# Low-part rotary scores as pairs of 64-row matmuls in a macaron attention kernel

## The chip, the core and the metric

The kernel runs on one core of one Trainium2 chip. The metric is the device time of one execution in microseconds, lower is better. Three runs of the kernel before gave 2384.84, 2382.19 and 2379.25 us, median 2382.19 us.

## What is computed

Four sequences of 512 tokens (width 1024) go through half a feed-forward block (a router over 8 experts with rank 16), an attention block, and half a feed-forward block again. The attention is of the latent kind: 32 heads, each query of 128 unrotated and 64 rotated dimensions, keys and values made from a latent of 128, one rotated key of 64 dimensions for all heads.

```python
q_pe = _apply_rope(q_pe, cos[None, :, None, :], sin[None, :, None, :])
k_pe = _apply_rope(k_pe, cos[None, :, :], sin[None, :, :])
scores = (jnp.einsum('bshd,bthd->bhst', q_nope, k_nope) + jnp.einsum('bshd,btd->bhst', q_pe, k_pe)) * scale
scores = jnp.where(causal[None, None], scores, jnp.finfo(scores.dtype).min)
probs = jax.nn.softmax(scores, axis=-1)
out = jnp.einsum('bhst,bthd->bshd', probs, v).reshape(b, s, NH * V_DIM)
```

## The kernel before

Every product is made from numbers split in a high and a low part (both fp32r), as high by high, high by low and low by high. The order of all work is written out by hand, for each engine in its own block, with counting semaphores between them.

The sequences are treated in two pairs (`p` = 0 and 1). For each pair, attention runs over 16 groups `g` of two heads. A group has four slots `k` = 0 to 3: `h = k % 2` is the head, `b = k // 2` the sequence of the pair. So there are 2 x 16 x 4 = 128 slots. Group 0 is written out in `first_body`, groups 1 to 14 are a loop over `body`, group 15 is `body` with `last`.

A slot computes scores for four query tiles `i` = 0 to 3 of 128 queries. Tile `i` is causal: it meets `(i + 1) * 128` keys, so its matmuls have 128, 256, 384 and 512 columns. It goes to PSUM bank `i % 2` (`bank_s`). Five matmuls make a tile: three for the unrotated part (`keyT`), and two for the rotated part (`ropeT`). For the rotated part, `qst` stacks the high part of the rotated query (64 rows) over its low part (64 rows), and `ropeT` holds the 64 rows of the key twice, so one matmul over 128 rows does high and low of the query against one part of the key. The first takes the key's high part, the second its low part. They are the fourth and fifth matmul of the tile, and both use the same weights.

Between the score tiles of slot `k`, TensorE does other work of the slot before it, in the order of `slot`: scores 0 and 1; the transposes of probabilities 0 and 1; output matmuls (six of 512 columns); scores 2; transposes 2; outputs; scores 3; transposes 3; projections ("fills"); outputs; values; outputs.

When a tile's scores are there, VectorE adds the mask on the diagonal (L1771) and takes the row maximum (L1773), and ScalarE takes the exponential out of the bank, with the row sum read by an accumulator instruction of its own that carries the semaphore `exp_done` (L1369). A score tile may start when its bank is free: tile `i` waits until the exponential of tile `i - 2` is done (L937). DVE's L1794 adds an output tile to the residual.

The stacked queries are made by DMA. After the rotation on GpSimd (`rope_r`), SyncE issues in `stack_halves` four DMAs, one per head and part, each 64 partitions by 512 numbers, into `qst[b]`. TensorE waits for them before scores 0 of slots 0 and 2 (`qst_in`).

In the profile the line of nearly all matmuls is that of a helper (L646, `products`); they are told apart by their tiles: `ps<-keyT,arena` and `ps<-ropeT,arena` are score matmuls.

Of the kernel before, what the change touches and what calls it, by code (L numbers as in the profile page):

```python
# [7 lines left out]
F32 = mybir.dt.float32  # L8
# [3 lines left out]
P = 128  # L12
# [5 lines left out]
def build_macaron(nc, x, wzkv, qnorm, kvnorm, wqn, wpe, wk, wv, wo, ra, rb, bm,  # L18
# [9 lines left out]
    SEQ = c_pos.shape[2]  # L28
    NPAIR = TOK // SEQ // 2
    NT = 2 * SEQ // P  # L30
# [8 lines left out]
    NG = NH // 2  # L39
# [19 lines left out]
    NF = [NT, 2 * NT, NT]  # L59
    U0 = [0, 2 * NT, 5 * NT]  # L60
# [22 lines left out]
    with ExitStack() as ctx:  # L83
        def sb(name, shape, dt=F32):
            return ctx.enter_context(nc.sbuf_tensor(name, shape, dt))

        def sem(name):
            return ctx.enter_context(nc.semaphore(name))
# [4 lines left out]
        ropeT = sb("ropeT", [P, 2, PAIR], F32R)  # L93
# [43 lines left out]
        rope_r = arena(W0 + 2 * QL, 2, SEQ)  # L137
# [4 lines left out]
        qst = [arena(X0, 2, SEQ), arena(8 * D, 2, SEQ)]  # L142
# [70 lines left out]
        def bank_s(i):  # L213
            return ps[:, i % 2, :]
# [32 lines left out]
        xt_hi = sem("xt_hi")  # L247
        xt_lo = sem("xt_lo")
# [30 lines left out]
        scores_done = sem("scores_done")  # L279
        masked = sem("masked")  # L280
        max_ready = sem("max_ready")
        exp_done = sem("exp_done")
# [11 lines left out]
        qst_in = sem("qst_in")  # L294
# [4 lines left out]
        y_added = sem("y_added")  # L299

        block = ctx.enter_context(nc.Block())
        GATE_STEPS = 13

        def lat_at(s, i):
# [16 lines left out]
        def slot_n(p, g, k):  # L321
            return (p * NG + g) * 4 + k

        def settle(eng):

            eng.sem_inc(settled, 1)
# [50 lines left out]
        def q_slot(p, g, k, first, last):  # L377

            if first and k < 2:
                a, d = PRO[p][f"q{k}"]  # L380
            elif k:
                a, d = q_events(p, last, first)[f"q{k}"]
            else:
                a, d = q_events(p, False)["q0"]
                a, d = a - EV[p], d - EVD[p]
            return qbase(p, g) + a + 1, qbase_d(p, g) + d + 1
# [23 lines left out]
        def _(sp):  # L410
# [124 lines left out]
            def swap_halves():  # L535
                for q in range(4):
                    o = q ^ 1
                    sp.dma_start(rope_f[32 * q:32 * q + 32, 1, :], rope_f[32 * o:32 * o + 32, 0, :])\
                      .then_inc(swap_in, 16)

            def stack_halves(n, b, used):
                sp.wait_ge(rope_ready, n + 1)
                settle(sp)
                if used is not None:
                    sp.wait_ge(scores_done, used)
                    settle(sp)
                for h in range(2):
                    for part in range(2):
                        dst = 64 * (part ^ h)
                        sp.dma_start(qst[b][dst:dst + 64, h, :].bitcast(F32),  # L550
                                     rope_r[64 * h:64 * h + 64, part, :].bitcast(F32)).then_inc(qst_in, 16)
                sp.wait_ge(qst_in, 64 * (n + 1))
                settle(sp)

            def attention(p):
# [86 lines left out]
        def _(pe):  # L642
# [7 lines left out]
            def three(w_hi, w_lo, m_hi_, m_lo_):  # L650
                return [(w_hi, m_hi_), (w_hi, m_lo_), (w_lo, m_hi_)]
# [273 lines left out]
            def scores(p, g, k, i, first, last):  # L925

                h, b = k % 2, k // 2
                n = slot_n(p, g, k)
                if i == 0:

                    a, d = q_slot(p, g, k, first, last)
                    pe.wait_ge(q_act, a)
                    pe.wait_ge(q_dve, d)
                    if h == 0:
                        pe.wait_ge(qst_in, 64 * (p * 2 * NG + 2 * g + b + 1))
                if not (first and k == 0 and i < 2):
                    pe.wait_ge(exp_done, 4 * n + i - 1)  # L937
                elif i == 0:

                    pe.wait_ge(xt_hi, U0[p] + NF[p] + NT)  # L940
                    pe.wait_ge(xt_lo, U0[p] + NF[p] + NT)
                qs = slice(i * P, (i + 1) * P)
                ks = slice(b * SEQ, b * SEQ + (i + 1) * P)
                dst = bank_s(i)[:, 0:(i + 1) * P]
                products(dst, three(qT[h][:, 0, qs], qT[h][:, 1, qs], keyT[:, 0, ks], keyT[:, 1, ks])
                         + [(qst[b][:, h, qs], ropeT[:, 0, ks]), (qst[b][:, h, qs], ropeT[:, 1, ks])])\
                    .then_inc(scores_done, 1)

            def turn_probs(n, k, i, first):

# [165 lines left out]
        def _(act):  # L1116
# [53 lines left out]
            def gates(c):  # L1170
                act.wait_ge(gate_chain, c * GATE_STEPS + 3)
                ts = slice((c % 2) * HT, (c % 2 + 1) * HT)
                nc.scalar.activation(lgt[:, 1, ts], lgt[:, 0, ts], ACT.Exp).then_inc(gate_exp, 1)
# [247 lines left out]
            def drained(p, s):  # L1421
                n = all_slots(p) - 1
                for i in range(NS):
                    turned(n, i)
                norm_ffn(s, 0)

                act.wait_ge(qst_in, 64 * (p + 1) * 2 * NG)
                split_ra(s)
                valued(n, 3)
                norm_ffn(s, 1)  # L1430
                turned_ffn(s, 0)

                act.wait_ge(y_done, y_n(p, NG, 1))
                turned_ffn(s, 1)
                norm_ffn(s, 2)
                for i in range(5):
                    keep_h(F0[s] + i)
                    turned_ffn(s, i + 2)
                    if i == 3:
                        gates((F0[s] + i) // HT)  # L1440
                    norm_ffn(s, i + 3)
                    if i == 0:
                        split_bm(s)
# [31 lines left out]
        def _(dve):  # L1475
# [31 lines left out]
            def gates(c, stage_):  # L1507

                first = (0, 3, 8, GATE_STEPS)
                step = [first[stage_]]  # L1510
                base = c * GATE_STEPS

# [406 lines left out]
        def _(pool):  # L1919
# [58 lines left out]
            def rotate(n, a_wait, first=False, between=None):  # L1978

                step = [4 * n]  # L1980

                def link(ins):
                    step[0] = step[0] + 1
                    ins.then_inc(rope_chain, 1)
                    pool.wait_ge(rope_chain, step[0])
                    settle(pool)
                pool.wait_ge(q_act, a_wait)
                settle(pool)
                if not first:

                    pool.wait_ge(qst_in, 64 * n)
                    settle(pool)
                link(G.tensor_tensor(rope_f[:, 2, :], rope_f[:, 0, :], pos_tab[:, 0, :], ALU.mult))  # L1993
                if between is not None:
                    between()
                pool.wait_ge(swap_in, 64 * (n + 1))
                settle(pool)
                link(G.tensor_tensor(rope_f[:, 1, :], rope_f[:, 1, :], pos_tab[:, 1, :], ALU.mult))  # L1998
                link(G.tensor_tensor(rope_r[:, 0, :], rope_f[:, 2, :], rope_f[:, 1, :], ALU.add))
                link(G.tensor_tensor(rope_f[:, 2, :], rope_f[:, 2, :], rope_f[:, 1, :], ALU.add))  # L2000
                G.tensor_tensor(rope_r[:, 1, :], rope_f[:, 2, :], rope_r[:, 0, :].bitcast(F32),
                                ALU.subtract).then_inc(rope_ready, 1)
# [111 lines left out]
```

## Time and profile before

| | |
|---|---|
| median of three runs | 2382.19 us |
| the profiled execution | 2382.79 us |
| its span, first to last instruction | 2380.7 us |
| mean granted TensorE clock | 0.989 |
| TensorE matmul busy | 2318.6 us (97%), 12832 matmuls |
| VectorE busy | 1627.7 us (68%) |
| ScalarE busy | 950.4 us (40%) |
| GpSimd busy | 521.3 us (22%) |
| score matmuls on `ropeT` | 1024 |
| DMAs that stack queries | 256, of 128 KB |

Matmul records overlap one another since matmuls are pipelined: how fast TensorE goes is read from the distance of starts, not from durations. PEld rows are the weight loads that belong to the matmuls, one each. A row of the timeline merges neighbours of one kind: its start is that of the first, its duration runs to the end of the last.

### The profile page before, as it was taken

Reading aid. Unit: us, or ns where it says so; the run is one execution under the profiler, and the core shown is the slowest. Engines: PE = TensorE matmul, PEld = TensorE weight load, DVE = VectorE, ACT = ScalarE, POOL = GpSimd, SP = SyncE. Lnnn points to the kernel's source line nnn. Section 1 sums busy time; section 2 is a strip of 40 time slices with the busy share of each in tenths; the row PEclk is TensorE's granted clock in tenths of the full one; section 3 lists DMA queues with packets and bytes.
Section 4 is the critical chain, followed back from the end, with each engine's and each line's share of the span. In section 5 each row is a group of like instructions: output and inputs, shape, how many; then the busy total and the mean of one; then the engine's idle time right before and its main releaser. Section 6 shows DMA issues by size and latency. Waiting matters only on the chain.

```text
span 2380.7 us, 40789 instructions
## 1 busy us (share of the span) xinstructions
PE 2318.6 (97%) x12832; PEld 1992.7 (84%) x12832; DVE 1627.7 (68%) x3581; ACT 950.4 (40%) x2311; POOL 521.3 (22%) x568
## 2 busy tenths in 40 slices
PE   8989999999999999999998989999999999999999
PEld 7977888888888888888888868888888888888888
DVE  6656666676666676666776556666666666666676
ACT  5533334443343344433444433333333333333343
POOL 4222221112222111222132222222222222222211
PEclk9999999999999999999999989999999999999999
DMA  4023333332223333333221212222222222222221
GB/s 150 17 68 108 107 103 102 106 97 80 95 74 97 105 104 106 107 107 95 96 90 64 66 44 79 78 78 78 78 78 78 78 78 78 78 78 78 75 67 72
DMA packets 101050, 203.45 MB, mean 85 GB/s; under 512 B 12544, under 2 KB 40704, under 8 KB 98944
## 3 DMA queue, kind: packets, MB, share of 16 engines
q1 hardware_dynamic: 79488, 156.55, 21.9%
q10 hardware_dynamic: 21504, 46.14, 5.9%
q8 instruction: 35, 0.57, 0.1%
q14 instruction: 23, 0.19, 0.0%
HBM read 97.78 MB, written 54.53 MB: 64 GB/s over the span
## 4 chain that ended last, share of the span: by engine, by line
PE 89%; DVE 3%; DMA 3%; ACT 2%; POOL 1%; issue 1%; SPq 1%; ACTq 0%; DVEq 0%; POOLq 0%
PE ps L646 74%; PE ps L956 6%; PE ps L714 4%; PE ps L915 2%; PE ps L660 1%; DVE arena L1477 1%; PE ps L921 1%; DMA kept_out<-arena 1%; ACT arena L1118 1%; PE ps L1086 1%; DVE stats L1486 1%; DMA out<-xacc 1%; DMA xacc<-in_x 0%; DMA arena<-arena 0%; DMA stage<-stage 0%
## 5 line engine op out<-in xcount | busy, mean ns | idle before, releaser
L646 PE MATMUL ps<-arena 128*128 128x512 f32 (+1 forms) x4032 | 966.7, 380 | 3.4 <-DVE arena L1477 1.5
L1477 DVE TENSOR_TENSOR arena<-ps,arena 128x384 fp32r<-128x384 f32 (+4 forms) x920 | 549.2, 601 | 508.8 <-ACT arena L1118 502.8
L1118 ACT ACTIVATE arena<-ps 128x384 fp32r<-128x384 f32 (+4 forms) x920 | 470.1, 527 | 868.6 <-PE ps L646 459.5
L646 PEld LDWEIGHTS ps<-arena 128*128 128x128 f32 x4032 | 677.1, 190 | 122.5 <-issue 9.4
L646 PE MATMUL ps<-zT,arena 128*128 128x512 f32 x1728 | 450.5, 405 | 2.8 <-issue 1.4
L1369 ACT ACTIVATE stage<-ps,negmax 128x128 f32<-128x128 f32 (+3 forms) x512 | 270.7, 529 | 366.4 <-DVE negmax L1773 362.5
L1794 DVE TENSOR_TENSOR xacc<-ps,xacc 128x512 f32<-128x512 f32 x512 | 351.7, 687 | 82.3 <-PE ps L646 73.8
L646 PEld LDWEIGHTS ps<-zT,arena 128*128 128x128 f32 x1728 | 318.5, 190 | 73.5 <-issue 3.8
L1993 POOL TENSOR_TENSOR stage<-stage,pos_tab 128x512 f32<-128x512 f32 x64 | 82.7, 1292 | 1294.7 <-ACT stage L1118 1287.7
L646 PE MATMUL ps<-keyT,arena 128*128 128x128 f32 (+3 forms) x1536 | 351.2, 337 | 9.0 <-ACT stage L1369 5.5
L646 PEld LDWEIGHTS ps<-keyT,arena 128*128 128x128 f32 x1536 | 260.7, 191 | 66.6 <-issue 22.4
L646 PEld LDWEIGHTS ps<-arena,lat 128*128 128x128 f32 x1536 | 247.5, 190 | 36.1 <-ACT arena L1118 5.9
L646 PE MATMUL ps<-arena,lat 128*128 128x512 f32 (+3 forms) x1536 | 260.6, 319 | 5.8 <-ACT arena L1118 5.1
L1773 DVE TENSOR_REDUCE negmax<-ps 128x1 f32<-128x128 f32 (+3 forms) x512 | 251.5, 491 | 17.5
L646 PE MATMUL ps<-ropeT,arena 128*128 128x128 f32 (+3 forms) x1024 | 247.5, 323 | 0.0
L956 PE MATMUL ps<-ident,stage 128*128 128x128 f32 x1280 | 203.6, 273 | 4.6 <-DVE arena L1477 3.7
L1771 DVE TENSOR_TENSOR ps<-ps,mask 128x128 f32<-128x128 f32 x512 | 150.7, 294 | 59.1 <-PE ps L646 59.1
L646 PEld LDWEIGHTS ps<-ropeT,arena 128*128 128x128 f32 x1024 | 174.0, 191 | 11.5
L956 PEld LDWEIGHTS ps<-ident,stage 128*128 128x128 f32 x1280 | 158.2, 141 | 28.5 <-DVE stage L1783 4.9
L1783 DVE TENSOR_SCALAR stage<-stage,rrec 128x128 f32<-128x128 f32 (+3 forms) x512 | 165.7, 388 | 4.5
L1998 POOL TENSOR_TENSOR stage<-stage,pos_tab 128x512 f32<-128x512 f32 x64 | 82.5, 1288 | 177.3 <-DMA stage<-stage 177.3
L714 PE MATMUL ps<-arena 128*128 128x288 f32 x768 | 110.7, 299 | 5.1 <-ACT stage L1118 2.7
(86 smaller groups left out, 1311.3 us busy)
## 6 DMA issues: line engine op xcount, KB each, us to landing
arena<-arena SPq DMA_DIRECT2D x256, 128.0 KB, 2.3
kept_out<-arena SPq DMA_DIRECT2D x16, 2048.0 KB, 6.3
arena<-kept_out ACTq DMA_DIRECT2D x32, 1024.0 KB, 5.6
stage<-stage SPq DMA_DIRECT2D x256, 64.0 KB, 2.0
stage<-in_wo SPq DMA_DIRECT2D x16, 1024.0 KB, 6.1
kept_q<-arena SPq DMA_DIRECT2D x16, 768.0 KB, 7.4
arena<-kept_q ACTq DMA_DIRECT2D x32, 384.0 KB, 3.1
out<-xacc SPq DMA_DIRECT2D x15, 512.0 KB, 2.7
```

The costliest lines, as they stand in the source:

```text
L646: last = nc.tensor.matmul(dst, w, m, start=start and n == 0, stop=stop and n == len(passes) - 1, skip_group_check=skip)
L714: last = nc.tensor.matmul(bzs[half], xnT[:, b, xp, k * P:(k + 1) * P], w_lat[:, wp, k, half * ZH:(half + 1) * ZH], start=(k == 0 and c == ...
L956: last = nc.tensor.transpose(bank_t(i)[:, j * P:(j + 1) * P], prob[:, k % 2, poff(i) + j * P:poff(i) + (j + 1) * P], ident[:, :])
L1118: return nc.scalar.activation(dst, src, ACT.Copy)
L1369: nc.scalar.activation(prob[:, k % 2, poff(i):poff(i + 1)], bank_s(i)[:, 0:(i + 1) * P], ACT.Exp, bias=negmax[:, k % 2, i:i + 1], accum_ou ...
L1477: return nc.vector.tensor_tensor(dst, src, part.bitcast(F32), ALU.subtract)
L1771: nc.vector.tensor_tensor(diagonal, diagonal, mask[:, :], ALU.add).then_inc(masked, 1)
L1773: nc.vector.tensor_reduce(negmax[:, k % 2, i:i + 1], bank_s(i)[:, 0:(i + 1) * P], AX_X, ALU.max, negate=True).then_inc(max_ready, 1)
L1783: nc.vector.tensor_scalar(pr, pr, rrec[:, k % 2, i:i + 1], None, ALU.mult).then_inc(prob_ready, 1)
L1794: nc.vector.tensor_tensor(xs, bank_y(j), xs, ALU.add).then_inc(y_added, 1)
L1993: link(G.tensor_tensor(rope_f[:, 2, :], rope_f[:, 0, :], pos_tab[:, 0, :], ALU.mult))
L1998: link(G.tensor_tensor(rope_f[:, 1, :], rope_f[:, 1, :], pos_tab[:, 1, :], ALU.mult))
```

## The change

The matmul with the key's low part is cut from 128 rows to 64: it takes only the high part of the query (low by low is no longer computed). For two neighbouring tiles `i` and `i + 1` the two 64-row matmuls are issued one behind the other, ahead of all else of the pair. One uses rows 0 to 63 of the array, the other rows 64 to 127. So that both find the query's high part in their rows, the DMAs that stack the queries swap the halves for odd query tiles; there are now eight DMAs, each of 64 partitions by two runs of 128 numbers, and `qst_in` counts to 128 for each stack. As both tiles of a pair are started at once, the even tile waits until both banks are free, that is for the exponential of tile `i - 1`, and the odd tile has no wait of its own.

```diff
+            def every_other(ap, odd):
+                return ap.bitcast(F32).rearrange("p (t o s) -> p t o s", o=2, s=P)[:, :, odd, :]
...
                 for h in range(2):
                     for part in range(2):
-                        dst = 64 * (part ^ h)
-                        sp.dma_start(qst[b][dst:dst + 64, h, :].bitcast(F32),
-                                     rope_r[64 * h:64 * h + 64, part, :].bitcast(F32)).then_inc(qst_in, 16)
-                sp.wait_ge(qst_in, 64 * (n + 1))
+                        for odd in range(2):
+                            dst = 64 * (part ^ h ^ odd)
+                            sp.dma_start(every_other(qst[b][dst:dst + 64, h, :], odd),
+                                         every_other(rope_r[64 * h:64 * h + 64, part, :], odd)).then_inc(qst_in, 16)
+                sp.wait_ge(qst_in, QST * (n + 1))
...
-                if not (first and k == 0 and i < 2):
-                    pe.wait_ge(exp_done, 4 * n + i - 1)
-                elif i == 0:
-                    pe.wait_ge(xt_hi, U0[p] + NF[p] + NT)
-                    pe.wait_ge(xt_lo, U0[p] + NF[p] + NT)
+                if i % 2 == 0:
+                    if not (first and k == 0 and i == 0):
+                        pe.wait_ge(exp_done, 4 * n + i)
+                    else:
+                        pe.wait_ge(xt_hi, U0[p] + NF[p] + NT)
+                        pe.wait_ge(xt_lo, U0[p] + NF[p] + NT)
+                    for o in range(2):
+                        rows = slice(64 * (h ^ o), 64 * (h ^ o) + 64)
+                        t = i + o
+                        nc.tensor.matmul(bank_s(t)[:, 0:(t + 1) * P], qst[b][rows, h, t * P:(t + 1) * P],
+                                         ropeT[rows, 1, b * SEQ:b * SEQ + (t + 1) * P], start=True, stop=False)
...
                 products(dst, three(qT[h][:, 0, qs], qT[h][:, 1, qs], keyT[:, 0, ks], keyT[:, 1, ks])
-                         + [(qst[b][:, h, qs], ropeT[:, 0, ks]), (qst[b][:, h, qs], ropeT[:, 1, ks])])\
-                    .then_inc(scores_done, 1)
+                         + [(qst[b][:, h, qs], ropeT[:, 0, ks])], start=False).then_inc(scores_done, 1)
```

On TensorE, in the loop body of pair 0, the stretch from scores 1 of a slot to scores 3 stands as follows before (L646 is a matmul of `products`, L956 a transpose, L937 the register of the wait for the bank):

```order
L646 MATMUL ps<-keyT,arena 128x256 x3
L646 MATMUL ps<-ropeT,arena 128x256 x2
L951 ISA
L953 REGISTER_ALU
L956 MATMUL ps<-ident,stage 128x128
L951 REGISTER_ALU
L956 MATMUL ps<-ident,stage 128x128 x2
L991 ISA
L646 MATMUL ps<-arena 128x512 x6
L937 REGISTER_ALU
L646 MATMUL ps<-keyT,arena 128x384 x3
L646 MATMUL ps<-ropeT,arena 128x384 x2
```

And the same stretch with the change (lines have moved: L957 is the new 64-row matmul, L654 `products`, L972 the transpose, L947 the register of the wait):

```order
L654 MATMUL ps<-keyT,arena 128x256 x3
L654 MATMUL ps<-ropeT,arena 128x256
L967 ISA
L969 REGISTER_ALU
L972 MATMUL ps<-ident,stage 128x128
L967 REGISTER_ALU
L972 MATMUL ps<-ident,stage 128x128 x2
L1007 ISA
L654 MATMUL ps<-arena 128x512 x6
L947 REGISTER_ALU
L957 MATMUL ps<-ropeT,arena 128x384
L957 MATMUL ps<-ropeT,arena 128x512
```

The fifth matmul of each tile has gone, and those of tiles 2 and 3 stand in front of tile 2's others, behind the wait.

On SyncE, in `first_body` of pair 0, the swaps of halves (`stage<-stage`), the loads of output weights and the two stacks (`arena<-arena`) stand before as:

```order
L538 DMA stage<-stage 32x512 x4
L445 DMA stage<-in_wv 128x2x128
L446 DMA stage<-in_wo 128x2x1024
L550 DMA arena<-arena 64x512 x4
L538 DMA stage<-stage 32x512 x4
L550 DMA arena<-arena 64x512 x4
L459 DMA kept_out<-arena 128x4096
```

and with the change as:

```order
L539 DMA stage<-stage 32x512 x4
L446 DMA stage<-in_wv 128x2x128
L447 DMA stage<-in_wo 128x2x1024
L558 DMA arena<-arena 64x2x128 x8
L539 DMA stage<-stage 32x512 x4
L558 DMA arena<-arena 64x2x128 x8
L460 DMA kept_out<-arena 128x4096
```

Eight issues stand for each stack where there were four, with half the bytes each.

## Rows read from the trace of the kernel before

**Rows 1.** The page, part 1: busy time, share, instructions.
```profile
PE 2318.6 (97%) x12832; PEld 1992.7 (84%) x12832; DVE 1627.7 (68%) x3581; ACT 950.4 (40%) x2311; POOL 521.3 (22%) x568
```

**Rows 2.** Groups by line and shape: busy us, mean ns; idle before.
```profile
L646 PE MATMUL ps<-ropeT,arena 128*128 128x512 f32 x256 | 80.9, 397 | 0.0
```

**Rows 3.** Timeline, one slot's score tiles: start us, us, what.
```profile
1569.10 0.39 PE L646 MATMUL ps<-ropeT,arena 128*128 128x128 f32 x2
1569.32 0.57 PE L646 MATMUL ps<-keyT,arena 128*128 128x256 f32 x3
...
1569.73 0.39 PE L646 MATMUL ps<-ropeT,arena 128*128 128x256 f32 x2
...
1569.96 0.49 PE L956 MATMUL ps<-ident,stage 128*128 128x128 f32 x3
...
1570.20 1.64 PE L646 MATMUL ps<-arena 128*128 128x512 f32 x6
...
1571.68 0.68 PE L646 MATMUL ps<-keyT,arena 128*128 128x384 f32 x3
...
1572.20 0.51 PE L646 MATMUL ps<-ropeT,arena 128*128 128x384 f32 x2
...
1572.55 0.49 PE L956 MATMUL ps<-ident,stage 128*128 128x128 f32 x3
...
1574.96 0.63 PE L646 MATMUL ps<-ropeT,arena 128*128 128x512 f32 x2
...
1575.44 0.60 PE L956 MATMUL ps<-ident,stage 128*128 128x128 f32 x4
```

**Rows 4.** Timeline of the same slot: VectorE, ScalarE, and tile 2's first load.
```profile
1569.02 0.69 DVE L1794 TENSOR_TENSOR xacc<-ps,xacc 128x512 f32<-128x512 f32 x1
...
1569.63 0.29 DVE L1771 TENSOR_TENSOR ps<-ps,mask 128x128 f32<-128x128 f32 x1
...
1569.95 0.29 DVE L1773 TENSOR_REDUCE negmax<-ps 128x1 f32<-128x128 f32 x1
...
1570.16 0.30 DVE L1771 TENSOR_TENSOR ps<-ps,mask 128x128 f32<-128x128 f32 x1
...
1570.49 0.42 DVE L1773 TENSOR_REDUCE negmax<-ps 128x1 f32<-128x256 f32 x1
...
1570.95 0.48 ACT L1369 ACTIVATE stage<-ps,negmax 128x256 f32<-128x256 f32 x1 [0.22 <-DVE negmax L1773]
1571.32 0.19 ACT L1369 ACTIVATION_READ_ACCUMULATOR stage<-ps,negmax 128x1 f32 x1
...
1571.45 0.59 PEld L646 LDWEIGHTS ps<-keyT,arena 128*128 128x128 f32 x3
```

**Rows 5.** Timeline, the same place in slot 3 of pair 0.
```profile
320.05 0.19 ACT L1369 ACTIVATION_READ_ACCUMULATOR stage<-ps,negmax 128x1 f32 x1
...
320.84 0.19 PEld L646 LDWEIGHTS ps<-keyT,arena 128*128 128x128 f32 x1 [0.24 <-issue]
```

**Rows 6.** Timeline near the end: six matmuls, a load among them held up.
```profile
2373.93 1.56 PE L646 MATMUL ps<-arena 128*128 128x512 f32 x6
...
2374.74 0.53 PEld L646 LDWEIGHTS ps<-arena 128*128 128x128 f32 x3 [0.16 <-DVE xacc L1578]
```

**Rows 7.** Part 6 of the page: DMA issues, count, KB, us to landing.
```profile
arena<-arena SPq DMA_DIRECT2D x256, 128.0 KB, 2.3
```

**Rows 8.** Timeline of the stack DMAs, steady state.
```profile
1559.24 2.43 SPq L550 DMA_DIRECT2D arena<-arena  x4
```

**Rows 9.** Timeline of a stack in the first group of pair 0, and the load that needs it.
```profile
165.37 2.42 SPq L550 DMA_DIRECT2D arena<-arena  x4
170.41 0.19 PEld L646 LDWEIGHTS ps<-keyT,arena 128*128 128x128 f32 x1 [0.24 <-issue]
```

**Rows 10.** Timeline of a stack in the second group, and the matmul that needs it.
```profile
229.82 2.41 SPq L550 DMA_DIRECT2D arena<-arena  x4
```

**Rows 11.** Timeline of TensorE behind it.
```profile
235.18 0.55 PE L646 MATMUL ps<-keyT,arena 128*128 128x128 f32 x3 [1.64 <-DMA arena<-arena]
```

More of the change, by code:

```diff
@@ L301, in build_macaron @@
         block = ctx.enter_context(nc.Block())
+        QST = 128
         GATE_STEPS = 13
@@ L934, in scores @@
                     if h == 0:
-                        pe.wait_ge(qst_in, 64 * (p * 2 * NG + 2 * g + b + 1))
-                if not (first and k == 0 and i < 2):
-                    pe.wait_ge(exp_done, 4 * n + i - 1)
-                elif i == 0:
-                    pe.wait_ge(xt_hi, U0[p] + NF[p] + NT)
-                    pe.wait_ge(xt_lo, U0[p] + NF[p] + NT)
+                        pe.wait_ge(qst_in, QST * (p * 2 * NG + 2 * g + b + 1))
+                if i % 2 == 0:
[9 more added lines that the diff above has]
+                                         ropeT[rows, 1, b * SEQ:b * SEQ + (t + 1) * P], start=True, stop=False)
                 qs = slice(i * P, (i + 1) * P)
@@ L1425, in drained @@
                 norm_ffn(s, 0)
-                act.wait_ge(qst_in, 64 * (p + 1) * 2 * NG)
+                act.wait_ge(qst_in, QST * (p + 1) * 2 * NG)
                 split_ra(s)
@@ L1989, in rotate @@
                 if not first:
-                    pool.wait_ge(qst_in, 64 * n)
+                    pool.wait_ge(qst_in, QST * n)
                     settle(pool)
```

## The prediction

> **What bounds the kernel now.** I read part 1 of the page first. TensorE's matmuls are busy for 97% of the span, VectorE comes next with 68% [rows 1]. So a matmul that is taken out counts, and a stall of TensorE counts in full. The groups by line and shape come next: there are four groups of score matmuls on the rotated key, for 128, 256, 384 and 512 columns, with 256 instances each, and the last stands in [rows 2]. Two for each tile in 128 slots make 256. The half with the key's low part, 128 of each size, is what the change works on. Durations in that view overlap (397 ns for 512 columns), so what a matmul costs I take from distances of starts in the timeline of one slot. Two of 128 columns: 1569.10 to 1569.32, 0.11 us each. Two of 256: 1569.73 to 1569.96, 0.115 each. Two of 384: 1572.20 to 1572.55, 0.175 each. Two of 512: 1574.96 to 1575.44, 0.24 each [rows 3]. Note that 128 and 256 columns cost the same: there the weight load is the pace, 0.11 us for each. Last I read what VectorE and ScalarE do between the second and third score tile [rows 4], since the change makes the third wait for them, and the DMAs that stack the queries [rows 7 to 11].
>
> **The pairs themselves.** No matmul goes away: five loads and five matmuls for a tile stay. The gain can only come from two 64-row matmuls running side by side.
>
> Tiles 2 and 3: before, 0.175 + 0.24 = 0.415 us for the two low parts. The trace of before holds no 64-row matmul, so I bound. Fully side by side, the pair costs its longer one, 0.24, and 0.175 is saved. If the second starts one load pace (0.11) behind the first, it costs 0.35, and 0.065 is saved. If they run one behind the other nothing is saved; that is a rival below. Between the first two I have no nearer row for either, and take the middle, 0.12. Times 128 slots: 15.4 us, from 8.3 to 22.4.
>
> The Trainium skill, "TensorE: Matmul & The Clock Gate", section "Measured speedup vs the span model", gives a pack of row tiles the duration of one matmul plus some 4 ns for each further tile. By it the pair would cost 0.244 us and the gain would be 0.171 x 128 = 21.9 us, near my upper end. No row of before can show it.
>
> Tiles 0 and 1: both are paced by loads, and both loads remain. 0 to 0.11 us for a slot, but only where it can be kept: it brings tile 2 forward by as much, and tile 2 now has to wait (next part). So it counts only in slot 3 of pair 0, 16 slots, where a fill stands in between: 16 x 0.055 = 0.9 us, from 0 to 1.8.
>
> **The new wait.** Tile 2 used to need the exponential of tile 0; now it needs that of tile 1. Queued behind the waiting load is all of TensorE. In the timeline the chain to that exponential is tight: an addition of the output before (L1794) starts at 1569.02 when its matmuls are done, and from there VectorE goes without a gap: mask 1569.63, maximum 1569.95, mask 1570.16, maximum 1570.49; then the exponential 1570.95, and its accumulator read 1571.32 to 1571.51, which carries the semaphore. Tile 2's first load starts at 1571.45 and its matmul at 1571.68 [rows 3, 4]. So the load comes 0.06 us before what it will have to wait for. A handover costs about 0.04 (maximum over at 1570.91, exponential at 1570.95), so the load moves to about 1571.55, 0.10 late. Does that move the matmul? The six output matmuls before it started at 1570.20 and are streaming until then. Near the end of the kernel a load among six such matmuls was held up so that its engine idled 0.16 us, and the six still took 1.56 us, which is five paces of 0.234 and one duration of 0.39 [rows 6]: it was hidden. So I take nearly nothing, 0.025 us. The other bound: after the wait the load's full lead of 0.23 (1571.45 to 1571.68) is needed again, the matmul starts at 1571.78, 0.10 late. In slot 3 of pair 0 the read ends at 320.24 and the load starts at 320.84 [rows 5], a margin of 0.6. That leaves 112 slots: 2.8 us, from 0 to 11. And what tiles 0 and 1 gain there is waited away, since VectorE's chain starts from the output before and does not move.
>
> Tile 0 now waits for tile 3 of the slot before, whose scores start at about 1575 in a slot that begins at 1569, some 7 us ahead of the next slot: no cost. VectorE, ScalarE and GpSimd do the same work as before.
>
> **The stacks.** Each stack has eight issues for four. Four take 2.43 us, so eight take 4.9, and the last starts some 2.5 us later. Bytes are the same. In steady state the last issue starts about 1.8 us after 1559.24, lands 2.3 us later at about 1563.4, and is needed just before 1569.1: margin over 5 us, nothing lost [rows 3, 7, 8]. In the first groups it is not so. Issued from 165.37, a stack lands at about 169.5 and is needed at 170.41, a margin of 0.9 [rows 7, 9]; the next stack has the same. Each then comes 1.6 us late. The one after, issued at 229.82, already holds TensorE for 1.64 us until 235.18 [rows 10, 11], and one at the start of pair 1 does so too: 2.5 us late each. TensorE has nothing to put there, since its order is fixed. 2 x 1.6 + 2 x 2.5 = 8.2 us, lost. I keep 6 to 12 as bounds, since shorter runs of 512 bytes may land later.
>
> **Changing between 128 and 64 rows.** There are four changes in a slot (into the pair and out of it, twice), 512 in all. The nearest row for none is the change from matmul to transpose at 1569.96, at the common pace of 0.11 [rows 3]: price 0. The nearest row for a dear one is the load in [rows 5], before which the load engine idled 0.24 us for nothing the profile shows, behind a matmul of another kind: 0.24 less the pace of 0.11 is 0.13 for each, 66 us in all. I take 0 in the sum, because most neighbours of different kinds in the timeline follow at pace, and keep the rest as a rival.
>
> **The sum.** -15.4 - 0.9 + 2.8 + 8.2 = -5.3 us, against the profiled execution's 2382.79, which lies 0.6 above the median of the runs: 2377.5, or 2377 against the median. Its own range, with all bounds to one side: 2382.8 - 22.4 - 1.8 + 6 = 2365, and 2382.8 - 8.3 + 11 + 12 = 2397.
>
> **The rivals.**
>
> A toll at each change of rows, which makes it slower. The engine must empty before matmuls of another row count go in, or the load can't be fetched ahead of it. For it speaks only [rows 5]; against it, that changes of weights, tile and kind cost nothing elsewhere. At 0.08 us, two thirds of the bound, 512 x 0.08 = 41 us on top of the sum: 2418, from 2395 to 2443. From 0.01 us for each change it eats the gain, and from 0.02 the kernel is slower. The Trainium skill, "TensorEngine Tiling (Array Packing)", section "Key Properties", says that changing the tiling mode, unlike changing the tile, drains the engine; it gives no price, and the trace of before, with one mode throughout, cannot show it. That is the page that speaks against this change.
>
> The pair does not overlap, so the change doesn't do what it says: the sum without 15.4 and 0.9, that is 2382.8 + 11.0 = 2394.
>
> The wait is dearer. The scores of tile 0 now end as the sixth matmul of the slot and not the fifth, one pace of 0.11 later; if VectorE's chain starts from them rather than from the addition, the load is 0.21 late. Beyond about 0.12 a late load is no longer hidden, so it decides from there: 0.1 x 112 = 11 us more, 2389.
>
> **Chances.** A measurement of this kernel can tell 0.2%, or 4.8 us, from no change: faster is below 2377.4, slower above 2387.0.
> - The sum as worked out, 0.50: it lies on the border, so 0.29 faster, 0.17 same, 0.04 slower.
> - The toll, 0.31: 0.30 slower, 0.01 same.
> - No overlap, 0.08: all but 0.01 slower.
> - The dearer wait, 0.11: 0.02 faster, 0.03 same, 0.06 slower.
>
> Together 0.31 faster, 0.22 same, 0.47 slower. The likeliest single case is the first, so the time is 2377. For 8 in 10 the range must reach into the toll: 2364 to 2438.
>
> **What the new profile would show.** Right: the starts of the two 64-row matmuls of tiles 2 and 3 lie 0 to 0.11 us apart, and the next one on `keyT` comes 0.24 to 0.35 after the first; PEld shows idle time before the pair of tiles 2 and 3 in 112 slots, released by ScalarE's L1369, below 0.15 us each, but the matmul's start does not move; the waits for the stack DMAs grow from two to four or more, together by about 8 us; nothing idles at the first `keyT` load behind a pair. Wrong: a gap of some 0.1 us at each entry into and exit from a pair (toll), 0.4 us from the first to the end of the pair (no overlap), or TensorE idle before tile 2 by 0.1 us or more in most slots (dearer wait). The forecast fails if any of these three is there, or if the stacks in the first groups are late by much more than 2.5 us.

## The result: 3.4% slower, and the profile after

The changed kernel takes 2462.55 us (median of four runs, 2461.22 to 2465.67). The kernel before took 2383.15 beside it. The ratio is 1.0339, with a 95% interval of 1.0325 to 1.0354: 79 us slower. The forecast was 2377, its range ended at 2438, and the time lies outside it. Of the four cases the one called "a toll at each change of rows" came true, and it is dearer than I had let it be.

Part 1 and two lines of part 5 of the page after (L957 is the new 64-row matmul; the column behind the bar is busy us, mean ns, then idle time before it):

```profile
PE 2385.2 (97%) x12832; PEld 1945.0 (79%) x12832; DVE 1653.9 (67%) x3581; ACT 949.6 (39%) x2311; POOL 520.8 (21%) x568
...
L957 PEld LDWEIGHTS ps<-ropeT,arena 64*128 64x128 f32 x512 | 48.0, 184 | 118.9 <-issue 71.1
L957 PE MATMUL ps<-ropeT,arena 64*128 64x128 f32 (+3 forms) x512 | 114.0, 413 | 21.7 <-ACT stage L1385 11.0
```

The number of matmuls is that of [rows 1], and TensorE is again busy for 97% of a longer span. Busy shares do not show the loss, since the records of matmuls last longer than their distances: the last output matmul below has a record of 0.40 us, and the next matmul starts 0.32 us after it, so the record covers the gap. What shows the loss is 118.9 us of idle time of the load engine before just 512 loads. Before 226 of the 256 pairs it is one stretch of 0.36 us, 81 us in all. Before 16 more it is 0.76 us, 12 us in all: these are tiles 2 and 3 of slot 3 in pair 0, which stand behind a fill. The last 26 us are 12 stretches of 0.65 to 4.5 us in the first groups of both pairs, the waits for stacks among them.

The timeline of TensorE at tiles 0 and 1 of a steady slot of pair 1, which answers to [rows 3]:

```profile
1591.05 0.39 PE L654 MATMUL ps<-arena 128*128 128x512 f32 x1
1591.37 0.39 PE L957 MATMUL ps<-ropeT,arena 64*128 64x128 f32 x2
1591.69 0.55 PE L654 MATMUL ps<-keyT,arena 128*128 128x128 f32 x3
1592.08 0.27 PE L654 MATMUL ps<-ropeT,arena 128*128 128x128 f32 x1
1592.19 0.57 PE L654 MATMUL ps<-keyT,arena 128*128 128x256 f32 x3
1592.60 0.28 PE L654 MATMUL ps<-ropeT,arena 128*128 128x256 f32 x1
1592.72 0.49 PE L972 MATMUL ps<-ident,stage 128*128 128x128 f32 x3
```

and of tiles 2 and 3, with the last output matmul ahead:

```profile
1594.20 0.40 PE L654 MATMUL ps<-arena 128*128 128x512 f32 x1
1594.53 0.49 PE L957 MATMUL ps<-ropeT,arena 64*128 64x384 f32 x2
1594.95 0.78 PE L654 MATMUL ps<-keyT,arena 128*128 128x384 f32 x3
1595.58 0.34 PE L654 MATMUL ps<-ropeT,arena 128*128 128x384 f32 x1
1595.75 0.49 PE L972 MATMUL ps<-ident,stage 128*128 128x128 f32 x3
```

The rows of the pairs hold two matmuls in 0.39 and 0.49 us. In the groups by shape a single 64-row matmul of 256 columns has a mean of 386 ns and one of 512 columns 498 ns, so both of a pair start together. The side-by-side run works. But from the last output matmul to the pair pass 0.32 us where 0.234 is usual, and from the pair to the next matmul 0.32 and 0.42 us, where a single matmul of the longer size would take 0.11 and 0.24.

The loads of the same place:

```profile
1591.37 0.19 PEld L957 LDWEIGHTS ps<-ropeT,arena 64*128 64x128 f32 x2 [0.35 <-issue]
1591.69 0.41 PEld L654 LDWEIGHTS ps<-keyT,arena 128*128 128x128 f32 x3
```

Before, tile 2's first load starts at 1571.45, together with the last output matmul and 0.23 ahead of its own [rows 4]. Now each first load behind a change starts together with its own matmul. It is not fetched ahead, in either direction. So a change costs twice: the load comes later behind the matmul before it than the next matmul usually would, and then it stands uncovered. That it waits until the array is empty is how I read the first part; the experiment with one 64-row matmul in each tile bears on it. From the starts of single matmuls in the two traces, from the last output matmul to the first transpose: tiles 0 and 1 took 1.37 us together and take 1.67; tile 2 took 1.10 and takes 1.55; tile 3, which has lost a matmul, took 1.40 and takes 1.17. Together 0.5 us more for a slot.

Waits of the load engine, and TensorE's waits for the stacks (us in total, times, longest):

```profile
PEld ps L957 <- issue: 71.1, 147, 4.5
PEld ps L654 <- issue: 64.0, 237, 1.6
PEld ps L957 <- ACT stage L1385: 45.8, 108, 2.4
...
PEld ps L654 <- DVE arena L1493: 9.2, 28, 0.4
```

```profile
PE ps L957 <- DMA arena<-arena: 10.8, 4, 4.3
```

The third line needs care. The profile puts 45.8 us to the exponential that a pair waits for. Here is that read, and the pair's load:

```profile
1594.09 0.19 ACT L1385 ACTIVATION_READ_ACCUMULATOR stage<-ps,negmax 128x1 f32 x1
...
1594.53 0.19 PEld L957 LDWEIGHTS ps<-ropeT,arena 64*128 64x128 f32 x2 [0.36 <-ACT stage L1385]
```

The read is over at 1594.28 and the load starts only at 1594.53, 0.25 us later, whereas a handover costs 0.04. The load at tiles 0 and 1, whose semaphore was there long before (`[0.35 <-issue]`), comes just as long after the output matmul: 0.32 against 0.33. So the idle time is named after the last semaphore, and would be there without it.

### The profile page after: what moved, and what is told of

Same layout as the page of the kernel before. It is cut to its first block, busy times and chain, and to the rows that moved or that the text cites. A ratio compares the mean times of both kernels' runs of the same rounds, so it can differ in the third digit from the quotient of the medians.

```text
span 2459.4 us, 41129 instructions
## 1 busy us (share of the span) xinstructions
PE 2385.2 (97%) x12832; PEld 1945.0 (79%) x12832; DVE 1653.9 (67%) x3581; ACT 949.6 (39%) x2311; POOL 520.8 (21%) x568
## 4 chain that ended last, share of the span: by engine, by line
PE 87%; DVE 4%; DMA 2%; ACT 2%; POOL 1%; SPq 1%; issue 1%; ACTq 0%; DVEq 0%; POOLq 0%
PE ps L654 70%; PE ps L972 5%; PE ps L722 4%; PE ps L957 4%; PE ps L923 2%; DVE arena L1493 2%; PE ps L668 1%; ACT arena L1134 1%; PE ps L929 1%; SPq L558 1%; DVE stats L1502 1%; DMA xacc<-in_x 1%; DMA stage<-stage 0%; ACT stage L1148 0%; DMA out<-xacc 0%
## 5 line engine op out<-in xcount | busy, mean ns | idle before, releaser
L654 PE MATMUL ps<-arena 128*128 128x512 f32 (+1 forms) x4032 | 967.1, 381 | 3.9 <-DVE arena L1493 1.5
L654 PEld LDWEIGHTS ps<-arena 128*128 128x128 f32 x4032 | 677.6, 190 | 123.0 <-issue 9.7
L654 PE MATMUL ps<-zT,arena 128*128 128x512 f32 x1728 | 449.2, 404 | 5.3 <-issue 2.8
L654 PEld LDWEIGHTS ps<-zT,arena 128*128 128x128 f32 x1728 | 317.7, 190 | 80.2 <-DVE arena L1493 9.2
L654 PE MATMUL ps<-keyT,arena 128*128 128x128 f32 (+3 forms) x1536 | 365.4, 351 | 0.0
L654 PEld LDWEIGHTS ps<-keyT,arena 128*128 128x128 f32 x1536 | 241.9, 191 | 76.4 <-issue 47.1
L654 PEld LDWEIGHTS ps<-arena,lat 128*128 128x128 f32 x1536 | 246.5, 189 | 33.5 <-issue 4.2
L654 PE MATMUL ps<-arena,lat 128*128 128x512 f32 (+3 forms) x1536 | 259.3, 318 | 3.3 <-ACT arena L1134 1.9
L972 PE MATMUL ps<-ident,stage 128*128 128x128 f32 x1280 | 204.6, 274 | 4.5 <-DVE arena L1493 3.7
L972 PEld LDWEIGHTS ps<-ident,stage 128*128 128x128 f32 x1280 | 159.8, 141 | 28.3 <-DVE stage L1799 4.7
L654 PE MATMUL ps<-ropeT,arena 128*128 128x128 f32 (+3 forms) x512 | 167.0, 326 | 0.0
L957 PEld LDWEIGHTS ps<-ropeT,arena 64*128 64x128 f32 x512 | 48.0, 184 | 118.9 <-issue 71.1
L957 PE MATMUL ps<-ropeT,arena 64*128 64x128 f32 (+3 forms) x512 | 114.0, 413 | 21.7 <-ACT stage L1385 11.0
```

Of the source, the lines that this page charges most:

```text
L654: last = nc.tensor.matmul(dst, w, m, start=start and n == 0, stop=stop and n == len(passes) - 1, skip_group_check=skip)
L957: nc.tensor.matmul(bank_s(t)[:, 0:(t + 1) * P], qst[b][rows, h, t * P:(t + 1) * P], ropeT[rows, 1, b * SEQ:b * SEQ + (t + 1) * P], start=T ...
L972: last = nc.tensor.transpose(bank_t(i)[:, j * P:(j + 1) * P], prob[:, k % 2, poff(i) + j * P:poff(i) + (j + 1) * P], ident[:, :])
```

## The experiments

All ratios are against the kernel before on the same chip, with 95% intervals; its median beside the first four experiments was 2381.48 us, beside the next three 2381.53, and beside the last two 2382.26 and 2382.16. "Loop of pair 0" is the time for a group of four slots, worked out from the starts of the first `keyT` matmul of group 3 and group 15, divided by 12: 64.47 before, 66.97 with the change. The same in pair 1: 59.43 and 61.47.

**Full rows.** The changed kernel with 128-row matmuls in the place of the 64-row ones.

```diff
-                        rows = slice(64 * (h ^ o), 64 * (h ^ o) + 64)
+                        rows = slice(0, P)
```

> The changed kernel, with its order, waits and eight stack DMAs, but the moved low-part matmuls use all 128 rows again, so no matmul has another row count than its neighbours. My theory (each change of row count empties the engine and leaves the next weight load uncovered, some 0.2 us for each of 512 changes): the toll goes with the 64 rows; what is left over the kernel before are the stacks, about 8 us, and a wait that a late load hides: 2390 to 2397 us, and the load engine idles less than 0.15 us before tile 2. Rival A (the order and the new wait for the exponential, to which the profile puts 45.8 us of idle time of the load engine, are the cost): it stays above 2430. Rival B (the 64-row matmuls do not run together): it would lose nothing by this edit against the changed kernel, 2450 to 2470, since tile 3 has a matmul less anyway.

Measured: 2404.24 us, ratio 1.0093 (1.0078 to 1.0109). The 64 rows carry 58 of the 79 us, and rival A falls. But 22.8 us are left, not 8 to 15, so the forecast for this run was missed by 7 us. The place of the wait, in the timeline of this kernel:

```profile
1593.62 1.64 PE L654 MATMUL ps<-arena 128*128 128x512 f32 x6
1595.00 0.30 PEld L957 LDWEIGHTS ps<-ropeT,arena 128*128 128x128 f32 x2 [0.17 <-ACT stage L1385]
1595.10 0.58 PE L957 MATMUL ps<-ropeT,arena 128*128 128x384 f32 x2
```

From the six output matmuls to the next pass 1.48 us, as before (1570.20 to 1571.68 [rows 3]). The load engine has idled 0.17 us before it, a little more than the 0.15 of the forecast, and the matmul is not late. Rival B falls too.

**The DMAs alone.** The kernel before with the eight stack DMAs.

```diff
-                        dst = 64 * (part ^ h)
-                        sp.dma_start(qst[b][dst:dst + 64, h, :].bitcast(F32),
-                                     rope_r[64 * h:64 * h + 64, part, :].bitcast(F32)).then_inc(qst_in, 16)
...
+                        for odd in range(2):
+                            dst = 64 * (part ^ h ^ odd)
+                            sp.dma_start(every_other(qst[b][dst:dst + 64, h, :], odd),
+                                         every_other(rope_r[64 * h:64 * h + 64, part, :], odd)).then_inc(qst_in, 16)
...
```

> The kernel before, with only the stack DMAs of the change: eight of 64 KB for four of 128 KB, halves swapped for odd tiles, which 128-row matmuls do not mind. My theory: 2.5 us later for each stack, which costs only in the first groups, 7 to 9 us in all: 2390 to 2392. Rival (runs of 512 bytes disturb or delay more than that in the steady state): above 2397. Rival (a loss in the first groups is made up later): 2383 to 2385.

Measured: 2391.87 us, ratio 1.0046 (1.0032 to 1.0060), 10.4 us. TensorE's waits for stacks in it:

```profile
PE ps L652 <- DMA arena<-arena: 10.1, 4, 4.1
```

These are four waits of 10.1 us in all, where there were two of 3.4 us, one of them that of [rows 11]: 6.7 us more. Both loops run at their old 64.47 and 59.43 us. From the first score to the start of the fourth group this trace takes 3.5 us more in pair 0 and 2.9 us more in pair 1. So what the trace shows of the loss, 6.4 us, is in the first groups. The profiled execution (2388.14 us) is the fastest of five, and the median lies 3.7 us above it; the two slowest have a granted clock of 0.986 against its 0.989. Where the rest of the 10.4 us arises, no trace shows.

**Both of a pair in the same half.**

```diff
-                        rows = slice(64 * (h ^ o), 64 * (h ^ o) + 64)
+                        rows = slice(64 * h, 64 * h + 64)
```

> The changed kernel, but both matmuls of a pair use the same 64 rows, so they cannot run side by side (for the odd tile these rows hold the low part of the query, so another part of the sum is computed). As many changes of row count as in the changed kernel. My theory: inside one row count the second load is covered and matmuls follow at the usual pace, so the pair gets longer by one load pace 0.11 us (tiles 0 and 1) and by one matmul of 384 columns, 0.17 us (tiles 2 and 3): 0.28 x 128 = 36 us more, 2490 to 2505 us; starts inside the pair 0.11 and 0.17 us apart instead of 3 ns. Rival (the pair does not really overlap in the changed kernel, starts are only stamped together): 2460 to 2466, no difference. Rival (a second tile in use costs too): below 2480.

Measured: 2497.84 us, ratio 1.0490 (1.0474 to 1.0506), 35.3 us above the changed kernel; the forecast was 36. The two pairs in its timeline:

```profile
1595.97 0.49 PE L957 MATMUL ps<-ropeT,arena 64*128 64x128 f32 x2
...
1596.39 0.55 PE L654 MATMUL ps<-keyT,arena 128*128 128x128 f32 x3
...
1599.24 0.67 PE L957 MATMUL ps<-ropeT,arena 64*128 64x384 f32 x2
...
1599.83 0.79 PE L654 MATMUL ps<-keyT,arena 128*128 128x384 f32 x3
```

0.42 and 0.59 us from pair to next, against 0.32 and 0.42: side by side saves 0.10 and 0.17 us. One detail of the forecast was off: the starts inside the pairs are 0.17 and 0.28 us apart and not 0.11 and 0.17, since the record of the first matmul begins with its uncovered load. And since this kernel has full rows' order and waits and nothing side by side, its distance to full rows is the toll by itself: 2497.84 - 2404.24 = 93.6 us, 0.183 us for each of 512 changes. In the loops, where nothing else waits, it is 0.194: (68.07 - 64.96) / 16 in pair 0 and (62.60 - 59.49) / 16 in pair 1. The first three groups of pair 0 take only 3.4 us more than with full rows in the traces, and not 3 x 3.1; there TensorE waits for stacks as well.

**96 rows.** The pair's matmuls on rows 0 to 95, not split in halves.

```diff
-                        rows = slice(64 * (h ^ o), 64 * (h ^ o) + 64)
+                        rows = slice(0, 96)
```

> The changed kernel, but the moved matmuls use 96 rows of the array, 0 to 95, for both tiles, so they do not use all rows but are issued as matmuls of the full array (for the odd tile other terms are summed). My theory, the toll is for leaving the full-array form and not for idle rows: as with all 128 rows, 2390 to 2397 us. Rival (any matmul with fewer active rows than its neighbour pays): 2455 or more, with two full matmuls one behind the other even 2490.

Measured: 2404.27 us, ratio 1.0095 (1.0080 to 1.0110), the time of full rows (2404.24) well within the noise; the loops agree too, 64.97 and 59.49 us against 64.96 and 59.49. So 32 idle rows cost nothing, and going to 64 rows does. The range I gave was missed by the same 7 us as in full rows.

**One 64-row matmul in each tile.** The kernel before, in its order.

```diff
-                         + [(qst[b][:, h, qs], ropeT[:, 0, ks]), (qst[b][:, h, qs], ropeT[:, 1, ks])])\
+                         + [(qst[b][:, h, qs], ropeT[:, 0, ks]),
+                            (qst[b][64 * h:64 * h + 64, h, qs], ropeT[64 * h:64 * h + 64, 1, ks])])\
```

> The kernel before in order, waits and stack DMAs, but the fifth matmul of each score tile uses only the 64 rows that hold the high part of the query. Nothing runs side by side, and each of the 512 tiles goes to 64 rows and back: 1024 changes of row count, twice those of the changed kernel. My theory: each change costs what the first runs gave, (2497.8 - 2404.2) / 512 = 0.18 us, so 2382 + 187 = 2569 us, 2555 to 2590. Rival (the toll hangs on a matmul that starts in another half of the rows or on a pair, not on the change of row count): below 2480. Rival (the toll is for time waited before a pair, since a pair starts behind a wait): below 2420.

Measured: 2534.42 us, ratio 1.0646 (1.0626 to 1.0667). 153 us for 1024 changes, 0.149 each. Both rivals fall, but the time is 21 us below the theory's range: the price of a change is not the same everywhere. The timeline at tiles 0 and 1:

```profile
1591.56 0.53 PE L646 MATMUL ps<-ropeT,arena 128*128 128x128 f32 x2
1592.02 0.61 PE L646 MATMUL ps<-keyT,arena 128*128 128x256 f32 x3
1592.47 0.59 PE L646 MATMUL ps<-ropeT,arena 128*128 128x256 f32 x2
1592.99 0.55 PE L957 MATMUL ps<-ident,stage 128*128 128x128 f32 x3
```

and at tile 3:

```profile
1598.40 0.82 PE L646 MATMUL ps<-ropeT,arena 128*128 128x512 f32 x2
...
1598.72 0.18 PEld L646 LDWEIGHTS ps<-ropeT,arena 64*128 64x128 f32 x1 [0.36 <-issue]
1599.14 0.42 PEld L957 LDWEIGHTS ps<-ident,stage 128*128 128x128 f32 x4 [0.24 <-issue]
1599.15 0.66 PE L957 MATMUL ps<-ident,stage 128*128 128x128 f32 x4
```

The entry is 0.32 again, 0.09 above the usual 0.234. Behind matmuls of 128, 256 and 384 columns it is 0.21, 0.21 and 0.26 us, where 0.11, 0.11 and 0.17 are usual: again 0.09 more. So this part of the price does not depend on how long the matmul before is, which fits a load that waits until the array is empty.

I compare starts with those of the kernel before, tile by tile, as medians of 28 slots in the loop of pair 1. Tile 0, the one whose exit leads to products, takes 0.29 us more; tiles 1, 2 and 3, whose exits lead to transposes, take 0.34 us more each. Together this is 1.31 us for a slot, and the loop shows the same, (64.68 - 59.43) / 4 = 1.31. Two changes of the pairs above cost 2 x 0.194 = 0.39 in the loops. For tiles 1 to 3 the difference of 0.05 can be read from the trace: behind an exit to transposes the second load comes 0.06 us after the first, behind the pairs' exits to products 0.108, so less of the load is uncovered. Tile 0 is cheaper by 0.10. A part of this may be that a 128-column matmul is paced by loads: at the pace of 512 columns it would take 0.234 / 4 = 0.06 us, as an estimate, and usually takes 0.11, so that 0.05 us of the emptying is free. Both explanations were formed afterwards and not tried on their own.

**A pair only for tiles 2 and 3.** In the changed kernel; tiles 0 and 1 as before.

```diff
-                if i % 2 == 0:
+                if i == 2:
...
+                if i < 2:
+                    products(dst, three(qT[h][:, 0, qs], qT[h][:, 1, qs], keyT[:, 0, ks], keyT[:, 1, ks])
+                             + [(qst[b][:, h, qs], ropeT[:, part, ks]) for part in range(2)]).then_inc(scores_done, 1)
...
```

> The changed kernel with the pair only for tiles 2 and 3; tiles 0 and 1 have five 128-row matmuls each again, in the order before. 256 changes of row count. My theory: 256 x 0.18 = 47 us of toll, less what running side by side gives, about 0.17 x 128 = 22 us, plus 10 us for the stacks and up to 12 us for order and wait: 2417 to 2432. Rival (the toll is paid mostly at the small tiles, whose matmuls are too short to hide a load): near 2405. Rival (mostly at the large pair): 2440 or more.

Measured: 2424.91 us, ratio 1.0188 (1.0171 to 1.0205), in the middle of the range. With half the changes it loses 43 us, about half of the 79, although this pair has the larger gain. Even it does not pay: in the loops a slot takes 0.21 to 0.22 us more than with order alone (the last experiment), (65.80 - 64.95) / 4 and (60.35 - 59.47) / 4, which is the toll of two changes, 0.39, less the gain of 0.17.

**Each pair twice.**

```diff
-                    for o in range(2):
+                    for o, again in ((0, True), (1, True), (0, False), (1, False)):
...
-                                         ropeT[rows, 1, b * SEQ:b * SEQ + (t + 1) * P], start=True, stop=False)
+                                         ropeT[rows, 1, b * SEQ:b * SEQ + (t + 1) * P], start=True, stop=again)
```

> The changed kernel, with each pair of 64-row matmuls issued twice, the second time overwriting the first with the same numbers. As many changes of row count as in the changed kernel, but twice the 64-row matmuls. My theory (the cost is at the change, and inside 64 rows loads are hidden behind matmuls as ever): a further pair costs its longer matmul, 0.11 + 0.235 us for a slot, 44 us in all: 2500 to 2515 us. Rival A (a 64-row load is never hidden behind a 64-row matmul, so 64 rows are dear wherever they stand): a further pair costs load and matmul, 0.22 + 0.32 us, 69 us in all: 2525 to 2540. Rival B (every pair is dear as a whole, 0.52 and 0.62 us): 2600 or more.

Measured: 2502.98 us, ratio 1.0518 (1.0500 to 1.0535), 40.4 us above the changed kernel, forecast 44. At tiles 2 and 3:

```profile
1601.96 0.30 PEld L957 LDWEIGHTS ps<-ropeT,arena 64*128 64x128 f32 x4 [0.36 <-ACT stage L1385]
1601.97 0.73 PE L957 MATMUL ps<-ropeT,arena 64*128 64x384 f32 x4
1602.63 0.47 PEld L654 LDWEIGHTS ps<-keyT,arena 128*128 128x128 f32 x3 [0.37 <-issue]
```

Four loads lie within 0.30 us while the first two matmuls run, and four matmuls take 0.66 us to the next, where two took 0.42. So between 64-row matmuls loads are fetched ahead as ever, a further pair costs its longer matmul (0.35 us for a slot in the loops, (68.35 - 66.97) / 4), and the price is all at the change.

**The waits alone.** The kernel before; tiles 0 and 2 wait for both banks.

```diff
-                    pe.wait_ge(exp_done, 4 * n + i - 1)
+                    pe.wait_ge(exp_done, 4 * n + i - (i % 2))
```

> The kernel before, with only the waits of the change: tiles 0 and 2 wait for both banks (the exponential of the tile just before), all matmuls and DMAs as before. It divides the 12 us by which the kernel with full rows is slower than the one with only the eight DMAs. My theory, read from the traces: half of that, 7 us, is not the wait but tile 3, which has a matmul less behind its outputs, so that the next fill comes 0.23 us too early for VectorE's read of its bank, in two slots of each group of pair 0. Here tile 3 keeps its matmul, so this is absent; what is left are the first groups, where little work stands between tiles: 2384 to 2389 us, and the loop of pair 0 at 64.47 us a group as before. Rival (the wait for the exponential itself costs the 12 us): 2392 to 2395, and the loop at 64.9 us a group.

Measured: 2385.15 us, ratio 1.0017 (1.0007 to 1.0027), 2.9 us. The loop of pair 0 takes 64.50 us, that of pair 1 59.47, against 64.47 and 59.43: 0.01 us for a slot, about 1 us in all. The first groups of pair 0 take 2.8 us more than before in this trace. The wait is nearly free.

**Order alone, tiles 2 and 3.** Both low parts with 128 rows ahead of tile 2, four stack DMAs.

```diff
+                if i == 2:
+                    pe.wait_ge(exp_done, 4 * n + i)
+                    for o in range(2):
+                        rows = slice(0, P)
...
```

> The kernel before with its four stack DMAs; only tiles 2 and 3 are changed in order: both low-part matmuls, with all 128 rows, stand ahead of tile 2, and tile 2 waits for the exponential of tile 1. What is disputed is the 9 us that the kernel with full rows loses beyond DMAs and wait. My theory: moving tile 3's matmul forward by itself is the cost, since the fill behind tile 3 then comes 0.23 us too early for VectorE in two slots of each group of pair 0; the loop of pair 0 takes 64.9 to 65.0 us a group and not 64.47, 7 us in all, with 3 us for the wait: 2390 to 2394. Rival (the loss comes with tiles 0 and 1, whose scores are ready later): 2383 to 2387 and 64.47 us a group.

Measured: 2388.84 us, ratio 1.0030 (1.0019 to 1.0042), 6.7 us; 1.2 us below the range I gave. But the loop of pair 0 takes 64.95 us, as forecast and as in full rows (64.96), 0.49 more than before without rounding, while the loop of pair 1 hardly moves (59.47). The place is the fill behind tile 3, in the timeline of the kernel with full rows:

```profile
857.04 1.93 PEld L654 LDWEIGHTS ps<-zT,arena 128*128 128x128 f32 x9 [0.29 <-DVE arena L1493]
```

Tile 3 has a matmul less between two fills that share a bank; the second then waits for VectorE to read the first. The kernel with order alone has 28 such waits, two for each group of the loop:

```profile
PEld ps L646 <- DVE arena L1487: 9.2, 28, 0.4
```

The changed kernel shows the same 28 waits with 9.2 us, and the kernel before shows none. What tile 3 saves is given back there.

## Why the prediction was wrong, step by step

**Changing between 128 and 64 rows: the failed step.** The prediction took 0 for each change "because most neighbours of different kinds in the timeline follow at pace", and let the rival reach 0.13 at the most. Measured it is 0.183, 93.6 us in all, and 0.194 in the loops. Both bounds came from rows that did not bear on it. A change from product to transpose and a load behind a matmul of another number format keep all 128 rows. The 0.24 us of idle time in [rows 5] looked alike but is another thing: the load there starts at 320.84, together with the second of two fill matmuls, so it is fetched ahead as ever, and its engine idled because these two matmuls stand 0.43 us apart. The true price of an entry is the 0.32 us from matmul to load plus an uncovered load of 0.107, less the usual 0.234, that is 0.19. The mechanism was named, given 0.31, and put beside a page of the Trainium skill, "TensorEngine Tiling (Array Packing)", section "Key Properties", that says it outright; the trace now agrees with that page, with the first load behind a change 0.32 us after the last matmul in place of 0.234 ahead of its own. The mistake was to let silence in a trace that had only one mode count against it. The time of 2377 belonged to the likeliest single case; the chances themselves had slower (0.47) ahead of faster (0.31), but the range stopped at a toll of about 0.12.

**The pairs themselves: right mechanism, too small.** I took 15.4 + 0.9 us, with upper bounds of 22.4 + 1.8; it is 35.3. Both loads of a pair are issued together, so tiles 2 and 3 save 0.17 (my upper bound), and tiles 0 and 1 save 0.10. I had counted the latter as waited away. In the changed kernel it is not: the read that tile 2 waits for is over 0.25 us before the pair's load starts, so the wait lies within the toll. What tiles 0 and 1 would save without a toll, no run shows. The Trainium skill, "TensorE: Matmul & The Clock Gate", section "Measured speedup vs the span model", counts some 4 ns for each further tile. The trace agrees: in all 256 pairs the second matmul starts 3 to 4 ns after the first.

**The new wait: right in size, partly by luck.** I took 2.8 us, it is 2.9 by the medians and 4.0 by the ratio, whose interval is 1.7 to 6.4. A load that is 0.1 us late hardly delays its matmul, as [rows 6] had said. But I had put the 2.8 us into 112 steady slots, 0.025 each, and the loops show 0.01 for a slot, about 1 us; the rest lies in the first groups, which I had not counted.

**The stacks: right mechanism, nearly the size.** 8.2 us forecast within 6 to 12, 10.4 measured. The waits went from two to four, all in the first groups, with nothing in the loops, as forecast; they grew by 6.7 us with the DMAs alone and by 7.4 in the changed kernel (3.4 to 10.8).

**Not seen at all: tile 3's gap.** The prediction asked what waits for tile 2, not who had used tile 3's fifth matmul as cover. In the loop of pair 0 it costs 0.49 us for each of 14 groups, 7 us. The kernel with order alone is 6.7 us slower with the wait included; the start of pair 1 is 4 us shorter in it, and its clock records have 40 us at half clock where the kernel before has 56, so the medians do not divide this further.

The account in medians: stacks 10.4, waits and order together 6.7, rest of full rows 5.7, toll 93.6, side by side -35.3: 81 us against 79 measured. That it closes is no check: the terms are differences of neighbouring kernels, and the 2 us left are those between the two medians of the kernel before (2383.15 and 2381.48). The 5.7 us are open. In full rows the first groups of pair 0 take 7.7 us more than with the DMAs alone, and the clock records of its trace hold 66 us at half clock against 56 in both the kernel before and the one with the DMAs alone. Longer stops at the start may have cost clock there; no run separates it.

No version here beats the kernel before. For a slot the pairs give 0.28 us, and four changes take 0.73 over the whole kernel and 0.78 in the loops.

## What to carry to other kernels

A matmul on half the rows among matmuls on all rows is not a cheaper matmul. It is a change of the array's form, and the change is paid at both ends (0.29 to 0.39 us for both, as measured here). Count changes before counting what is saved: at 0.18 to 0.19 us each, a stretch of paired 64-row matmuls must save some 0.37 us to break even; as an estimate, with pairs of 512 columns (0.234 us saved by each) that is two pairs in a row. Where a trace has no instance of a thing, its absence is no evidence for a price of zero, and the idle time that a profile names after a semaphore should be held against the same place without that wait.

## What the runs showed of the hardware that was not expected

- No weight load is fetched ahead across a change of form; within either form it is (loads start with the matmul before them, 0.234 us ahead of their own among 512-column matmuls). Behind a change the load and its own matmul are stamped some 2 ns apart.
- Entering 64 rows holds the load back by 0.09 us beyond the usual distance, whether the matmul before it has 128, 256, 384 or 512 columns; the rest of the price of an entry is the uncovered load, 0.107 us.
- The loads for two halves of the array go in parallel: stamped 3 ns apart, with the two matmuls behind them 3 to 4 ns apart.
- 96 active rows cost what 128 do (2404.27 against 2404.24 us), with no toll.
- Leaving for a transpose uncovers less of the load than leaving a pair for a product, 0.06 against 0.108 us.
- A load before which its engine idled 0.17 us, behind a 512-column matmul, delays nothing (1.48 us for the six matmuls ahead, with and without).
